# The last tile of a mixture of experts: its inner values in halves, its outputs in two transfers

## The chip, the cores and the metric

The kernel runs on one core of a Trainium2 chip. The metric is the device time of one execution in microseconds; three runs of the kernel before gave a median of 1152.88 us (1152.04 to 1154.29).

## The reference

A transformer block on x, 8 x 112 tokens of 512 channels. First x + tanh(g) * attention(layernorm(x)) with self and cross attention in simulated fp8, then a mixture of eight experts of which every token takes two:

```python
x = x + jnp.tanh(g_ffn[0]) * _L0_ffn_ref(_layernorm(x, axis=-1), Wr, Wg, Wu, Wd)

def _L0_ffn_ref(x, Wr, Wg, Wu, Wd):
    probs = jax.nn.softmax(x @ Wr, axis=-1)
    topk_w, topk_idx = jax.lax.top_k(probs, K)            # K = 2 of E = 8
    topk_w = topk_w / jnp.sum(topk_w, axis=-1, keepdims=True)
    for i in range(E):
        sel = topk_idx == i
        w_i = jnp.sum(topk_w * sel.astype(x.dtype), axis=-1, keepdims=True)
        h = jax.nn.silu(x @ Wg[i]) * (x @ Wu[i])
        output = output + w_i * (h @ Wd[i])
    return output
```

## The kernel before

The program has two parts: attention (up to about 790 us), and the projection with the experts. The change is in the second, in its last ten microseconds.

The 896 tokens with two choices each give 1792 rows. They are sorted by expert into tiles of 128 rows. How many tiles an expert fills depends on the routing, so the program runs TI = 21 tiles (2 x 7 + 8 - 1), enough for any routing. Rows that hold no token read token 0 when gathered, and when added back carry an index beyond the last token, which the transfer leaves out (bounds_check).

Every tile i passes these steps, with fp32 values handled as a rounded half (hi) and a rest (lo) so that TensorE's fp32r products keep their precision:
- GpSimd gathers 128 rows (gather, L1496). TensorE transposes them into the PSUM bank p_x, ScalarE takes xh, TensorE subtracts it (rest_of_rows), ScalarE takes xl.
- TensorE makes the gate and up products into the banks pg and pu, 12 matmuls of 512 columns each: four blocks k, three pairs of halves (products, L1748). ScalarE evacuates them (gated, L1586; upward, L1592), GpSimd multiplies them to hf (product, L1505).
- turn_inner (L1735): TensorE transposes hf into p_h. inner_high (L1598): ScalarE takes hh. rest_of_inner (L1741): TensorE subtracts it. inner_low (L1604): ScalarE takes hl.
- products again: the down product from hh and hl into the bank pd.
- result (L1612): ScalarE scales pd by the row's gate into y, of which there are two (y lies in the tile p_cat).
- add (L1511): GpSimd issues an indirect DMA that adds 128 rows of y into the output in memory (compute_op add).

Two adds must not be in flight at once, since two tiles may hold the same token: add(i) waits for `added`, the semaphore of the transfers' landing, to reach 16 * i. The order of the work is written out by hand, engine by engine, and software-pipelined: while TensorE makes tile i's gate and up products, the down product of tile i - 1 comes between, and ScalarE runs result(i - 1) before inner_high(i). For the last tile nothing is left to fill the gaps. The last statement of GpSimd's queue waits for the landing of the last add, and with that the program ends.

Of the kernel before, what the change touches and what calls it, by code (L numbers as in the profile page):

```python
# [21 lines left out]
ALU = mybir.AluOpType  # L22
ACT = mybir.ActivationFunctionType
AX = mybir.AxisListType.X

P = 128
B, T, D = 8, 112, 512
# [7 lines left out]
NT = B * T  # L35
EX, FF = 8, 512
FB = FF // P
# [3 lines left out]
TI = 2 * TJ + EX - 1  # L41
# [1212 lines left out]
def projected_experts(nc, c, sb, ps, sem, x, wproj, catd, W, Wr, ident, mhalf, proj_scale, gate,  # L1254
# [19 lines left out]
    hi, lo, l_done = ffn.hi, ffn.lo, ffn.l_done  # L1274
# [12 lines left out]
    def w_half(half, m):  # L1287

        return half[m // KB % 2][:, m % KB, :]

    def catr(m):
        return flat((hi, lo)[m // 2 % 2][2][:, 0:KB, :])[:, m % 2 * NT:(m % 2 + 1) * NT]

# [25 lines left out]
    of_row = sb(c, "of_row", [P, 2, TI], U32)  # L1319
    gate_of = sb(c, "gate_of", [P, 2, TI])  # L1320
# [12 lines left out]
    minus = sb(c, "minus", [P, P], F32R)  # L1333
# [5 lines left out]
    y = in_odd(0, 2 * D, F32).rearrange("p (r d) -> p r d", r=2)  # L1339
    lane_hot = in_odd(4 * D, CH * P, BF16).rearrange("p (n l) -> p n l", n=CH)  # L1340
    at = 4 * D + CH * P
# [11 lines left out]
    sg, up_out, hf = (results.held[:, 2 * k * FF:2 * (k + 1) * FF].bitcast(F32) for k in range(3))  # L1353
    hh = sb(c, "hh", [P, D], F32R)
    hl = sb(c, "hl", [P, D], F32R)

    p_count, p_rank, pg, pu, pd, p_x, p_h = (acc[:, j, :] for j in range(TJ))
    p_where = p_row[:, 0:2 * TI]
    p_share = p_row[:, 64:64 + 3 * TI]

# [95 lines left out]
    @block.gpsimd  # L1456
    def _(pool):
        pool.iota(expert_no[:, :], pattern=[[1, EX]], base=0, channel_multiplier=0,
                  allow_small_or_imprecise_dtypes=True).then_inc(pool_self, 1)
        pool.iota(tile_no[:, :], pattern=[[1, TI]], base=0, channel_multiplier=0,  # L1460
                  allow_small_or_imprecise_dtypes=True).then_inc(pool_self, 1)
        pool.iota(lane_no[:, :], pattern=[[1, P]], base=0, channel_multiplier=0,
                  allow_small_or_imprecise_dtypes=True).then_inc(pool_self, 1)
        pool.iota(block_row[:, :], pattern=[[P, TJ]], base=0, channel_multiplier=0,
                  allow_small_or_imprecise_dtypes=True).then_inc(pool_self, 1)
        pool.iota(block_no[:, :, :], pattern=[[0, 2], [1, TJ]], base=1, channel_multiplier=0,
                  allow_small_or_imprecise_dtypes=True).then_inc(pool_self, 1)
        pool.iota(part_no[:, :], pattern=[[0, 1]], base=0, channel_multiplier=1,
                  allow_small_or_imprecise_dtypes=True).then_inc(pool_self, 1)
        pool.memset(le[:, :, :], 1.0).then_inc(pool_self, 1)  # L1470
        pool.memset(tri[:, :], 1.0).then_inc(pool_self, 1)
        pool.memset(ones_bf[:, :], 1.0).then_inc(pool_self, 1)
        pool.memset(ends[:, 0:1], 0.0).then_inc(pool_self, 1)
        pool.wait_ge(pool_self, 10)
        pool.affine_select(out=le[:, :, :], in_=le[:, :, :], compare_op=ALU.is_ge, fill=0.0, base=0,
                           pattern=[[1, EX], [-1, EX]], channel_multiplier=0).then_inc(pool_self, 1)
        pool.affine_select(out=tri[:, :], in_=tri[:, :], compare_op=ALU.is_gt, fill=0.0, base=0,
                           pattern=[[1, P]], channel_multiplier=-1).then_inc(pool_self, 1)

        pool.memset(block_row[:, 0:1], -1.0).then_inc(const_done, 1)  # L1480
        pool.wait_ge(pool_self, 12)
        pool.tensor_scalar(minus[:, :], ident[:, :], -1.0, None, ALU.mult).then_inc(const_done, 1)
        pool.tensor_copy(tri_bf[:, :], tri[:, :]).then_inc(const_done, 1)
        pool.tensor_copy(lane_bf[:, :], lane_no[:, :]).then_inc(const_done, 1)

        for j in range(TJ):
            one = slice(j, j + 1)
            pool.wait_ge(stat_done, j + 1)
            pool.tensor_tensor(rstd[:, one], mv[:, j, 1:2], mhalf[:, 0:1], ALU.pow).then_inc(rstd_pow, 1)
            pool.wait_ge(rstd_pow, j + 1)  # L1490
            pool.tensor_tensor(shift[:, one], mv[:, j, 0:1], rstd[:, one], ALU.mult).then_inc(rstd_done, 1)

        def gather(i):
            if i >= 3:
                pool.wait_ge(tx_rdy, i - 2)
            pool.indirect_dma_start(  # L1496
                out=xr[:, i % 3, :], out_offset=None, in_=normed[:, :],
                in_offset=bass.IndirectOffsetOnAxis(ap=of_row[:, 0, i:i + 1], axis=0)).then_inc(xr_in[i % 3], 16)

        def product(i):  # L1500
            pool.wait_ge(sg_done, i + 1)
            pool.wait_ge(up_done, i + 1)
            if i >= 1:
                pool.wait_ge(th_rdy, i)
            pool.tensor_tensor(hf[:, :], sg[:, :], up_out[:, :], ALU.mult).then_inc(hf_done, 1)  # L1505

        def add(i):
            pool.wait_ge(y_done, i + 1)
            if i >= 1:
                pool.wait_ge(added, 16 * i)  # L1510
            pool.indirect_dma_start(  # L1511
                out=tokens[:, :], out_offset=bass.IndirectOffsetOnAxis(ap=of_row[:, 1, i:i + 1], axis=0),
                in_=y[:, i % 2, :], in_offset=None, bounds_check=NT - 1, oob_is_err=False,
                compute_op=ALU.add).then_inc(added, 16)

        pool.wait_ge(normed_kept, 32)
        pool.wait_ge(row_done, 1)
        for i in range(3):
            gather(i)
        pool.wait_ge(row_done, 2)  # L1520
        pool.wait_ge(out_kept, 32)
        for i in range(TI):
            product(i)
            if i >= 1:
                add(i - 1)
            if i + 3 < TI:
                gather(i + 3)
        add(TI - 1)
        pool.wait_ge(added, 16 * TI)

    @block.scalar
    def _(act):
# [61 lines left out]
        def inner_high(i):  # L1594
            act.wait_ge(th_rdy, i + 1)
            if i >= 1:
                act.wait_ge(dn_rdy, i)
            act.activation(hh[:, :], p_h[:, :], ACT.Copy).then_inc(hh_done, 1)  # L1598

        def inner_low(i):  # L1600
            act.wait_ge(sh_rdy, i + 1)
            if i >= 1:
                act.wait_ge(dn_rdy, i)
            act.activation(hl[:, :], p_h[:, :], ACT.Copy).then_inc(hl_done, 1)  # L1604

        def result(i):
            act.wait_ge(dn_rdy, i + 1)
            if i == 0:
                act.wait_ge(gate_done, 1)
            if i >= 2:  # L1610
                act.wait_ge(added, 16 * (i - 1))
            act.activation(y[:, i % 2, :], pd[:, :], ACT.Copy, scale=gate_of[:, 0, i:i + 1]).then_inc(y_done, 1)  # L1612

        rows_high(0)
        rows_low(0)
        for i in range(TI):
            gated(i)
            if i >= 1:
                inner_low(i - 1)
            upward(i)  # L1620
            if i + 1 < TI:
                rows_high(i + 1)
                rows_low(i + 1)
            if i >= 1:
                result(i - 1)
            inner_high(i)
        inner_low(TI - 1)
        result(TI - 1)

    @block.tensor  # L1630
    def _(pe):
# [98 lines left out]
        def turn_inner(i):  # L1730
            pe.wait_ge(hf_done, i + 1)
            if i >= 1:
                pe.wait_ge(hl_done, i)
            for k in range(FB):
                mm = pe.matmul(p_h[:, k * P:(k + 1) * P], hf[:, k * P:(k + 1) * P], ident[:, :],  # L1735
                               start=(k == 0), stop=False, is_transpose=True, skip_group_check=True)
            mm.then_inc(th_rdy, 1)

        def rest_of_inner(i):
            pe.wait_ge(hh_done, i + 1)  # L1740
            pe.matmul(p_h[:, :], minus[:, :], hh[:, :], start=False, stop=True,  # L1741
                      skip_group_check=True).then_inc(sh_rdy, 1)

        def products(bank, a_hi, a_lo, n, at, ks):
            for k in ks:
                for m in range(3):
                    a, w = ((a_hi, hi), (a_hi, lo), (a_lo, hi))[m]
                    mm = pe.matmul(bank[:, :], a[:, k * P:(k + 1) * P],  # L1748
                                   w[n][:, bass.ds(at + k, 1), :].rearrange("p a f -> p (a f)"),
                                   start=(k == 0 and m == 0), stop=(k == KB - 1 and m == 2))  # L1750
            return mm
# [35 lines left out]
                products(pd, hh[:, :], hl[:, :], 2, at.pop(i - 1), (2, 3)).then_inc(dn_rdy, 1)  # L1787
            turn_inner(i)
        rest_of_inner(TI - 1)
        pe.wait_ge(hl_done, TI)  # L1790
        pe.wait_ge(y_done, TI - 1)
        products(pd, hh[:, :], hl[:, :], 2, at.pop(TI - 1), range(FB)).then_inc(dn_rdy, 1)

    @block.vector
    def _(v):
# [214 lines left out]
```

## Time and profile before

| | |
|---|---|
| median of three runs | 1152.88 us (1152.04 to 1154.29) |
| profiled execution, its own time | 1152.41 us |
| its span | 1150.7 us |
| TensorE busy | 1086.5 us (94%) |
| ScalarE busy | 699.6 us (61%) |
| GpSimd busy | 501.8 us (44%) |

The span reaches from the first to the last event of the execution; some 1.7 us of its time lie outside it. PE is TensorE, PEld its weight loads, ACT ScalarE, DVE VectorE, POOL GpSimd, SP SyncE. Busy shares are means over the whole span and say nothing of its end; there, the chain of waits and the timeline are to be read. A duration of GpSimd's DMA_INDIRECT is the time in which GpSimd works on the instruction, not that of the transfer. Matmuls are pipelined: the start of one lies closer to the start of the next than its duration.

### The profile page before, as it was taken

What the parts mean: (1) busy time and instruction counts of PE and PEld (TensorE: products, weight loads), DVE (VectorE), ACT (ScalarE), POOL (GpSimd) and SP (SyncE); (2) the same over time, 40 slices, a digit from 0 to 9 for tenths busy, and PEclk for the clock granted to TensorE, in tenths of its full rate; (3) what the DMA queues carried; (4) which work ended last, traced back from release to release, by engine and by line L of the source; (5) the groups of instructions that cost most, each with busy time, mean ns of one, the idle gap of its engine ahead of it and who ended that gap; (6) DMA issues with size and microseconds to landing.
All of it is one profiled execution on the core that took longest, in us unless ns stands there. A gap on an engine that the chain in (4) does not pass through costs nothing. (4 is left out here: it accounts for less than half of the span.)

```text
span 1150.7 us, 19517 instructions
## 1 busy us (share of the span) xinstructions
PE 1086.5 (94%) x5662; PEld 891.0 (77%) x5662; DVE 779.8 (68%) x1558; ACT 699.6 (61%) x2032; POOL 501.8 (44%) x571
## 2 busy tenths in 40 slices
PE   4599999999999999999999999998999779999996
PEld 3488788888888788888887888886888657777785
DVE  7988986977776896777697766677454774655000
ACT  7668878666878856888867656763241323434432
POOL 3445565445544454445544554452000125565432
PEclk8799999999999999999999999999999879999999
DMA  7221111142111214121114111112944347673310
GB/s 265 106 69 48 49 36 45 36 154 90 44 37 44 62 36 181 44 54 36 44 36 135 63 45 36 46 34 94 351 157 147 129 151 217 182 239 97 54 43 0
DMA packets 52819, 107.39 MB, mean 93 GB/s; under 512 B 6064, under 2 KB 27056, under 8 KB 51184
## 3 DMA queue, kind: packets, MB, share of 16 engines
q1 hardware_dynamic: 48016, 97.00, 25.8%
q0 software_dynamic: 4704, 9.18, 3.5%
q8 instruction: 49, 0.80, 0.3%
q14 instruction: 50, 0.41, 0.1%
HBM read 91.48 MB, written 16.52 MB: 94 GB/s over the span
## 5 line engine op out<-in xcount | busy, mean ns | idle before, releaser
L529 POOL TENSOR_TENSOR c_lo<-c_raw,c_hi 128x500 fp32r<-128x500 f32 x96 | 124.0, 1292 | 194.0 <-ACT c_hi L581 194.0
L523 POOL TENSOR_TENSOR rs<-va,mhalf 125x2 f32<-125x2 f32 (+1 forms) x180 | 200.7, 1115 | 14.2 <-POOL va L516 0.2
L516 POOL TENSOR_TENSOR va<-ss,epst 125x2 f32<-125x2 f32 (+1 forms) x180 | 60.9, 338 | 179.4 <-DVE ss L1078 101.3
L798 PE MATMUL bank<-w_hi,c_hi 128*125 128x512 f32 x384 | 120.0, 434 | 8.2 <-ACT w_hi L576 6.9
L771 PE MATMUL bank<-w_hi,xqs 128*128 128x512 f32 (+2 forms) x464 | 111.1, 362 | 11.6 <-DVE xqs L1070 11.6
L798 PE MATMUL bank<-w_hi,c_lo 128*125 128x512 f32 x384 | 105.7, 397 | 0.0
L798 PE MATMUL bank<-w_lo,c_hi 128*125 128x512 f32 x384 | 105.1, 395 | 0.1
L771 PE MATMUL bank<-w_lo,xqs 128*128 128x512 f32 (+2 forms) x464 | 101.2, 340 | 0.1
L664 ACT ACTIVATE work<-bank,nmax 112x375 f32<-112x375 f32 x128 | 73.6, 584 | 44.9 <-DVE nmax L1107 44.8
L842 PE MATMUL bank<-kxT,qxT 128*112 128x375 f32 x256 | 97.0, 480 | 0.0
L771 PEld LDWEIGHTS bank<-w_hi,xqs 128*128 128x128 f32 (+1 forms) x464 | 74.1, 189 | 18.1 <-issue 12.2
L798 PEld LDWEIGHTS bank<-w_hi,c_hi 128*125 128x125 f32 x384 | 67.0, 188 | 26.5 <-issue 7.1
L798 PEld LDWEIGHTS bank<-w_hi,c_lo 128*125 128x125 f32 x384 | 71.7, 187 | 18.6
L798 PEld LDWEIGHTS bank<-w_lo,c_hi 128*125 128x125 f32 x384 | 71.2, 186 | 18.8 <-DVE w_lo L434 0.8
L771 PEld LDWEIGHTS bank<-w_lo,xqs 128*128 128x128 f32 (+1 forms) x464 | 75.3, 187 | 11.3 <-DVE w_lo L434 0.8
L873 PE MATMUL bank<-work 125*128 125x224 f32 x384 | 83.1, 352 | 0.0
L1133 DVE TENSOR_TENSOR results<-bank,smg 128x448 bf16<-128x448 f32 x64 | 39.9, 623 | 52.9 <-PE bank L873 52.9
L626 ACT ACTIVATE nkx<-bank 125x256 f32<-125x256 f32 x96 | 38.8, 404 | 58.6 <-PE bank L798 58.6
L873 PEld LDWEIGHTS bank<-work 125*128 125x128 f32 x384 | 72.4, 189 | 0.3
L1107 DVE TENSOR_REDUCE nmax<-bank 112x1 f32<-112x375 f32 x128 | 69.2, 543 | 3.0 <-PE bank L842 0.2
L1511 POOL DMA_INDIRECT out<-p_cat,of_row x21 | 45.5, 2167 | 58.2 <-ACT p_cat L1612 48.8
L856 PEld LDWEIGHTS bank<-ident,work 112*125 112x125 f32 x384 | 51.8, 188 | 19.2 <-issue 13.3
(266 smaller groups left out, 2798.7 us busy)
## 6 DMA issues: line engine op xcount, KB each, us to landing
c_raw<-in_ctxT SPq DMA_DIRECT2D x96, 250.0 KB, 2.6
shared<-in_w_in SPq DMA_DIRECT2D x13, 1024.0 KB, 9.2
shared<-in_wproj SPq DMA_DIRECT2D x32, 256.0 KB, 4.3
raw_g<-in_Wg SPq DMA_DIRECT2D x8, 1024.0 KB
raw_u<-in_Wu SPq DMA_DIRECT2D x8, 1024.0 KB, 6.2
raw_d<-in_Wd SPq DMA_DIRECT2D x8, 1024.0 KB, 5.4
cat_scratch<-results SPq DMA_DIRECT2D x32, 224.0 KB, 2.0
shared<-cat_scratch SPq DMA_DIRECT2D x2, 1792.0 KB, 9.4
```

The costliest lines, as they stand in the source:

```text
L516: pool.tensor_tensor(va[0:rows, lo:hi], ss[0:rows, lo:hi], epst[0:rows, lo:hi], ALU.add).then_inc(va_done, 1)
L523: pool.tensor_tensor(rs[0:rows, lo:hi], va[0:rows, lo:hi], mhalf[0:rows, lo:hi], ALU.pow).then_inc(rs_done, 1)
L529: pool.tensor_tensor(flat(c_lo[:, k, :, :]), flat(c_raw[:, k, :, :]), flat(c_hi[:, k, :, :]).bitcast(F32), ALU.subtract).then_inc(cl_done, 1)
L664: act.activation(pcross[0:T, h, :], p_cross[0:T, h % 2, 0:TC], ACT.Exp, bias=nmax[0:T, 4 + h:5 + h], accum_out=lsum[0:T, 4 + h:5 + h]).the ...
L771: m = pe.matmul(out, xqs[:, n, k, 0:rows], (w_hi, w_lo)[i // KB][:, k, lo:lo + w], start=(i == 0), stop=(i == 2 * KB - 1))
L798: m = pe.matmul(bank[0:CT, :], a[:, ch, k, :], w[:, k, CKX:CV], start=(i == 0), stop=(i == 3 * KB - 1))
L842: pe.matmul(p_cross[0:T, h % 2, 0:TC], qxT[:, t[1] % 2, h, :], kxT[:, h // HPG, :], start=True, stop=True).then_inc(sx_rdy, 1)
L856: m = pe.transpose(p_tr[0:CT, 1 - h % 2, k * T:(k + 1) * T], pcross[0:T, h, k * CT:(k + 1) * CT], ident[0:T, 0:T])
L873: m = pe.matmul(out[:, HPG * T:2 * HPG * T], valx[0:CT, par, k, g * P:(g + 1) * P], flat(pcrossT[0:CT, k, HPG * g:HPG * (g + 1), :]), star ...
L1107: v.tensor_reduce(nmax[0:T, 4 + h:5 + h], p_cross[0:T, h % 2, 0:TC], AX, ALU.max, negate=True).then_inc(mx_done, 1)
L1133: v.tensor_tensor(results.y[lin(t) % 2][:, g * 4 * T:(g + 1) * 4 * T].rearrange("p (a t) -> p a t", t=T), out_bank(t, g)[:, 0:4 * T].rearr ...
L1511: pool.indirect_dma_start(out=tokens[:, :], out_offset=bass.IndirectOffsetOnAxis(ap=of_row[:, 1, i:i + 1], axis=0), in_=y[:, i % 2, :], in ...
```

## The change

It concerns the last tile, TI - 1 = 20, alone.

- inner_banks: the transposes of its four blocks go to two banks, the first two to p_h, the last two to p_x. hh, the subtraction and hl are done in two halves of 256 columns each.
- Its down product goes to the banks pg (columns 0 to 255) and pu (256 to 511), one after the other, with 12 matmuls of 256 columns for each. It waits for both halves of hl.
- result makes y in two halves, each when its bank is ready. The result of tile 19 no longer comes before hh of tile 20 but behind hl.
- GpSimd waits for the landing of the first 20 adds, and then issues two indirect adds, one for each half of the columns, the second with no wait for the first's landing, since they don't meet.

```diff
+    def inner_banks(i):
+
+        if i < TI - 1:
+            return ((p_h, slice(0, FF)),)
+        return ((p_h, slice(0, FF // 2)), (p_x, slice(FF // 2, FF)))
...
+    OUT_BANKS = ((pg, slice(0, D // 2)), (pu, slice(D // 2, D)))
...
-        add(TI - 1)
-        pool.wait_ge(added, 16 * TI)
+        pool.wait_ge(added, 16 * (TI - 1))
+        for n, (bank, cols) in enumerate(OUT_BANKS):
+            pool.wait_ge(y_done, TI + n)
+            pool.indirect_dma_start(
+                out=tokens[:, :], out_offset=bass.IndirectOffsetOnAxis(ap=of_row[:, 1, TI - 1:TI], axis=0),
+                in_=y[:, (TI - 1) % 2, cols], in_offset=None, bounds_check=NT - 1, oob_is_err=False,
+                element_offset=n * (D // 2), compute_op=ALU.add).then_inc(added, 16)
+        pool.wait_ge(added, 16 * (TI + 1))
...
-            act.activation(hh[:, :], p_h[:, :], ACT.Copy).then_inc(hh_done, 1)
+            for bank, cols in inner_banks(i):
+                act.activation(hh[:, cols], bank[:, cols], ACT.Copy).then_inc(hh_done, 1)
...
+            for n, (bank, cols) in enumerate(inner_banks(i)):
+                act.wait_ge(sh_rdy, i + 1 + n)
+                if i >= 1:
+                    act.wait_ge(dn_rdy, i)
+                act.activation(hl[:, cols], bank[:, cols], ACT.Copy).then_inc(hl_done, 1)
...
-            act.activation(y[:, i % 2, :], pd[:, :], ACT.Copy, scale=gate_of[:, 0, i:i + 1]).then_inc(y_done, 1)
+            if i < TI - 1:
+                act.activation(y[:, i % 2, :], pd[:, :], ACT.Copy, scale=gate_of[:, 0, i:i + 1]).then_inc(y_done, 1)
+                return
+            for n, (bank, cols) in enumerate(OUT_BANKS):
+                act.wait_ge(dn_rdy, TI + n)
+                act.activation(y[:, i % 2, cols], bank[:, cols], ACT.Copy,
+                               scale=gate_of[:, 0, i:i + 1]).then_inc(y_done, 1)
...
-            if i >= 1:
+            if 1 <= i < TI - 1:
                 result(i - 1)
             inner_high(i)
         inner_low(TI - 1)
+        result(TI - 2)
         result(TI - 1)
...
+            for n, (bank, cols) in enumerate(inner_banks(i)):
+                pe.wait_ge(hh_done, i + 1 + n)
+                pe.matmul(bank[:, cols], minus[:, :], hh[:, cols], start=False, stop=True,
+                          skip_group_check=True).then_inc(sh_rdy, 1)
...
-        pe.wait_ge(hl_done, TI)
-        pe.wait_ge(y_done, TI - 1)
-        products(pd, hh[:, :], hl[:, :], 2, at.pop(TI - 1), range(FB)).then_inc(dn_rdy, 1)
+        pe.wait_ge(hl_done, TI + 1)
+        for bank, cols in OUT_BANKS:
+            for k in range(FB):
+                for m in range(3):
+                    a, w = ((hh, hi), (hh, lo), (hl, hi))[m]
+                    mm = pe.matmul(bank[:, cols], a[:, k * P:(k + 1) * P],
+                                   w[2][:, bass.ds(at[TI - 1] + k, 1), cols].rearrange("p a f -> p (a f)"),
+                                   start=(k == 0 and m == 0), stop=(k == FB - 1 and m == 2))
+            mm.then_inc(dn_rdy, 1)
```

On ScalarE, the end of the queue before (results are the gate and up values, the two p_cat rows are y of tiles 19 and 20):

```order
L1592 ACTIVATE results<-p_acc 128x512 [waits hf_done,u_rdy]
L1612 ACTIVATE p_cat<-p_acc,gate_of 128x512 [waits added,dn_rdy]
L1598 ACTIVATE hh<-p_acc 128x512 [waits dn_rdy,th_rdy]
L1604 ACTIVATE hl<-p_acc 128x512 [waits dn_rdy,sh_rdy]
L1612 ACTIVATE p_cat<-p_acc,gate_of 128x512 [waits added,dn_rdy]
```

And in the changed kernel:

```order
L1605 ACTIVATE results<-p_acc 128x512 [waits hf_done,u_rdy]
L1612 ACTIVATE hh<-p_acc 128x256 [waits dn_rdy,th_rdy]
L1612 ACTIVATE hh<-p_acc 128x256
L1619 ACTIVATE hl<-p_acc 128x256 [waits dn_rdy,sh_rdy] x2
L1628 ACTIVATE p_cat<-p_acc,gate_of 128x512 [waits added,dn_rdy]
L1632 ACTIVATE p_cat<-p_acc,gate_of 128x256 [waits dn_rdy,added]
L1632 ACTIVATE p_cat<-p_acc,gate_of 128x256 [waits dn_rdy]
```

y of tile 19 (128x512) has moved from before hh to behind both halves of hl, and y of tile 20 has become two.

On GpSimd, the end of the queue before (out is the output, p_cat holds y; a DMA row shows the whole output's shape):

```order
L1505 TENSOR_TENSOR results<-results 128x512 [waits th_rdy,up_done,sg_done]
L1511 DMA out<-p_cat,of_row 896x512 [waits added,y_done2] x2
L100 UNCONDITIONAL_BRANCH [waits added]
```

And in the changed kernel:

```order
L1512 TENSOR_TENSOR results<-results 128x512 [waits th_rdy,up_done,sg_done]
L1518 DMA out<-p_cat,of_row 896x512 [waits added,y_done2]
L1538 DMA out<-p_cat,of_row 896x512 [waits y_done2,added]
L1538 DMA out<-p_cat,of_row 896x512 [waits y_done2]
L100 UNCONDITIONAL_BRANCH [waits added]
```

Behind the last hf there are three adds in place of two; the second waits for the landing of the one before (added), the third for its half of y alone.

## Rows read from the trace of the kernel before

**Rows 1.** The page: busy time, share of the span and instructions of each engine.

```profile
PE 1086.5 (94%) x5662; PEld 891.0 (77%) x5662; DVE 779.8 (68%) x1558; ACT 699.6 (61%) x2032; POOL 501.8 (44%) x571
```

**Rows 2.** Busy time by stretch: PE, PEld, DVE, ACT, POOL (instructions), TensorE clock, DMA share, GB/s.

```profile
1137.00:1145.70 8.70, 3.94 (x17) 2.52 (x15) 0.00 (x0) 2.46 (x4) 3.14 (x2) 0.98 0.01 0
1145.70:1150.70 5.00, 0.00 (x0) 0.00 (x0) 0.00 (x0) 0.00 (x0) 0.00 (x0) 0.50 0.01 0
```

**Rows 3.** The chain of waits at the end: start us, us, what.

```profile
1138.23 0.51 PE p_acc L1741
...
1138.76 0.61 ACT hl L1604
...
1139.49 3.06 PE p_acc L1748 x12
...
1142.57 0.70 ACT p_cat L1612
...
1143.32 0.72 issue
1144.04 1.57 POOL out L1511
```

**Rows 4.** DMA answer from 1138.4 us to the end: packets and bytes.

```profile
DMA packets 288, 0.00 MB, mean 0 GB/s; under 512 B 288, under 2 KB 288, under 8 KB 288
```

**Rows 5.** DMA answer from 1099.9 to 1109.7 us: queue, packets, MB, share.

```profile
q0 software_dynamic: 224, 0.51, 28.3%
```

**Rows 6.** Timeline of GpSimd: start us, us, engine, line, operation, [idle before, releaser].

```profile
1099.96 1.59 POOL L1511 DMA_INDIRECT out<-p_cat,of_row  x1 [3.03 <-ACT p_cat L1612]
...
1138.46 1.57 POOL L1511 DMA_INDIRECT out<-p_cat,of_row  x1 [2.26 <-ACT p_cat L1612]
1144.04 1.57 POOL L1511 DMA_INDIRECT out<-p_cat,of_row  x1 [4.01 <-ACT p_cat L1612]
```

**Rows 7.** Timeline of TensorE and ScalarE at the end.

```profile
1136.80 0.60 PE L1735 MATMUL p_acc<-ident,results 128*128 128x128 f32 x4
1137.00 0.69 ACT L1612 ACTIVATE p_cat<-p_acc,gate_of 128x512 f32<-128x512 f32 x1 [2.21 <-PE p_acc L1748]
...
1141.91 0.40 PE L1748 MATMUL p_acc<-lo_d,hh 128*128 x1
1142.14 0.39 PE L1748 MATMUL p_acc<-hi_d,hl 128*128 x1
```

**Rows 8.** Timeline of ScalarE: copies of 256 columns out of PSUM.

```profile
49.64 0.39 ACT L619 ACTIVATE val<-bank 112x256 f32<-112x256 f32 x1 [0.27 <-PE bank L771]
49.92 0.38 ACT L621 ACTIVATE nk<-bank 128x256 f32<-128x256 f32 x1
```

**Rows 9.** Timeline of TensorE: matmuls of 256 columns, four in a row.

```profile
322.68 0.64 PE L771 MATMUL bank<-w_lo,xqs 128*128 128x256 f32 x4
323.15 0.63 PE L771 MATMUL bank<-w_hi,xqs 128*112 128x256 f32 x4
```

**Rows 10.** Groups of weight loads by form: busy us, mean ns.

```profile
L771 PEld LDWEIGHTS bank<-w_lo,xqs 128*128 128x128 f32 x336 | 58.5, 192 | 11.3 <-DVE w_lo L434 0.8
...
L1748 PEld LDWEIGHTS p_acc<-hi_d,hh 128*128 128x128 f32 x84 | 15.8, 188 | 8.0 <-issue 6.0
```

**Rows 11.** Busy time by stretch, around the packets of tile 19's add.

```profile
1140.80:1140.90 0.10, 0.10 (x2) 0.10 (x1) 0.00 (x0) 0.00 (x0) 0.00 (x0) 1.00 0.07 1
1140.90:1141.00 0.10, 0.10 (x2) 0.05 (x2) 0.00 (x0) 0.00 (x0) 0.00 (x0) 1.00 0.00 0
```

**Rows 12.** Busy time by stretch, at the end of the first gather's packets.

```profile
925.20:925.40 0.20, 0.00 (x0) 0.00 (x0) 0.17 (x1) 0.00 (x0) 0.20 (x1) 0.50 0.27 103
```

**Rows 13.** Timeline of TensorE: what waited for the first gather.

```profile
925.89 1.11 PE L1721 MATMUL p_acc<-ident,shared 128*128 128x128 f32 x4 [5.20 <-DMA shared<-normed_rows,of_row]
```

**Rows 14.** Timeline of GpSimd: a gather right behind a gather.

```profile
923.83 0.95 POOL L1496 DMA_INDIRECT shared<-normed_rows,of_row  x1 [0.30 <-issue]
```

**Rows 15.** Timeline of GpSimd: an add that waited for the landing of another.

```profile
971.72 1.64 POOL L1511 DMA_INDIRECT out<-p_cat,of_row  x1 [1.97 <-DMA out<-p_cat,of_row]
```

More of the change, by code:

```diff
@@ L1597, in inner_high @@
                 act.wait_ge(dn_rdy, i)
-            act.activation(hh[:, :], p_h[:, :], ACT.Copy).then_inc(hh_done, 1)
+            for bank, cols in inner_banks(i):
+                act.activation(hh[:, cols], bank[:, cols], ACT.Copy).then_inc(hh_done, 1)
         def inner_low(i):
-            act.wait_ge(sh_rdy, i + 1)
-            if i >= 1:
-                act.wait_ge(dn_rdy, i)
-            act.activation(hl[:, :], p_h[:, :], ACT.Copy).then_inc(hl_done, 1)
+            for n, (bank, cols) in enumerate(inner_banks(i)):
[3 more added lines that the diff above has]
+                act.activation(hl[:, cols], bank[:, cols], ACT.Copy).then_inc(hl_done, 1)
         def result(i):
@@ L1623, in _ @@
                 rows_low(i + 1)
-            if i >= 1:
+            if 1 <= i < TI - 1:
                 result(i - 1)
@@ L1733, in turn_inner @@
                 pe.wait_ge(hl_done, i)
+            banks = inner_banks(i)
             for k in range(FB):
-                mm = pe.matmul(p_h[:, k * P:(k + 1) * P], hf[:, k * P:(k + 1) * P], ident[:, :],
-                               start=(k == 0), stop=False, is_transpose=True, skip_group_check=True)
+                bank = banks[k * len(banks) // FB][0]
+                mm = pe.matmul(bank[:, k * P:(k + 1) * P], hf[:, k * P:(k + 1) * P], ident[:, :],
+                               start=(k * len(banks) % FB == 0), stop=False, is_transpose=True,
+                               skip_group_check=True)
             mm.then_inc(th_rdy, 1)
         def rest_of_inner(i):
-            pe.wait_ge(hh_done, i + 1)
-            pe.matmul(p_h[:, :], minus[:, :], hh[:, :], start=False, stop=True,
-                      skip_group_check=True).then_inc(sh_rdy, 1)
+            for n, (bank, cols) in enumerate(inner_banks(i)):
+                pe.wait_ge(hh_done, i + 1 + n)
+                pe.matmul(bank[:, cols], minus[:, :], hh[:, cols], start=False, stop=True,
+                          skip_group_check=True).then_inc(sh_rdy, 1)
         def products(bank, a_hi, a_lo, n, at, ks):
```

## The prediction

> **What bounds the kernel now.** I began with the busy shares of the page [rows 1]: TensorE holds 94% of the span. The slices after 1137 us tell another story: TensorE is busy 3.94 of the 8.70 us from 1137.00 to 1145.70, and in the last 5.00 us no engine is busy at all [rows 2]. So the end of the program is a chain of hand-overs, and the change touches only that end. The chain of waits [rows 3] gives it step by step: TensorE's transposes of the last tile, ScalarE's hh (the rounded inner values), TensorE's remainder product, ScalarE's hl (the rest), twelve products on TensorE (3.06 us), ScalarE's scaled copy into y (0.70 us), 0.72 us in which GpSimd gets the indirect add under way, and 1.57 us of GpSimd for the add itself. That ends at 1145.61; the span ends at 1150.7, so 5.1 us follow, for the landing of the add and the end of the program.
>
> The DMA answer from 1138.4 us on [rows 4] is what decides the case. The last two adds together move 288 packets and 0.00 MB. With these inputs the last tiles hold no token, and their rows are out of bounds. The add of 1099.96 us, in whose stretch 0.51 MB were moved (half of it by a gather of 128 rows of 2 KB), still took 1.59 us of GpSimd, against 1.57 us for an empty one [rows 5, 6]. What is split at the end is therefore a fixed cost and no data.
>
> **The change part by part.** All times are on the axis of the profiled execution.
>
> *Inner values in halves.* The transposes end at 1137.40 [rows 7]; hh now follows at once, at 1137.44 (such a hand-over takes 0.02 to 0.04 us in the chain), since the scaled copy of tile 19, which held ScalarE from 1137.00, has moved behind hl. A copy of 256 columns takes 0.39 us, and the next starts 0.28 us after it [rows 8]. The halves of hh are thus 1137.44 to 1137.83 and 1137.72 to 1138.11. The remainder product takes 0.51 us at 512 columns from a standing start [rows 3]; streamed, one of 512 columns starts 0.23 us behind the last [rows 7] and one of 256 some 0.118 us (the next four start 0.47 us behind four) [rows 9], so I take 0.51 - 0.12 = 0.39. The first half of the rest is in PSUM at 1138.26, the second at 1138.54. Then hl: 1138.28 to 1138.67, and 1138.56 to 1138.95. Before, hl ended at 1139.36. This part brings the products forward by 0.4 us.
>
> *Products in two halves of columns.* They are 24 of 256 columns in place of 12 of 512: 24 x 0.118 = 2.83 us against 12 x 0.233 = 2.80 (the twelve of the chain with their slower first one: 3.06). From 1139.07 the first half is ready at about 1140.7 and the second at about 1142.15, against 1142.55 before. The products' weight loads show 0.188 us each, longer than 0.118, and each is preceded by register work for the weights' place; if that holds them to the old pace, the halves take 24 x 0.233 = 5.6 us, and the second is ready at about 1144.85. But the row of 256 columns carries loads of 0.192 us too [rows 10] and still keeps 0.118, so I take that.
>
> *Results of the last tile.* A scaled copy of 256 columns should take 0.69 - 0.60 + 0.39 = 0.48 us. The first half of y is ready at 1141.2, the second at 1142.65, against 1143.26 before.
>
> *The result of tile 19 is moved.* This is the step that costs. It ran at 1137.00; now it stands behind both copies of hl, so it starts at 1138.84 and y is ready at 1139.53, 1.84 us later than 1137.69. GpSimd starts an add 0.77 us after y (1143.27 to 1144.04 [rows 3]; 1137.69 to 1138.46 [rows 6, 7]), so the add of tile 19 is on GpSimd from 1140.30 to 1141.87, where it was from 1138.46 to 1140.03.
>
> *The wait for the adds.* GpSimd waits for the landing of the add of tile 19 before it issues the first half for tile 20. Before, this was hidden: the add's last packet is seen by 1140.9, 0.87 us after GpSimd was done [rows 11], and the next y came at 1143.26. Now GpSimd frees itself at 1141.87 and y (first half) has long been there at 1141.2, so the landing is what ends last. Its length is not in the trace. From below it is 0.87 us; the first gather shows up to 0.5 us more, since its packets thin out by 925.4 and TensorE starts on it at 925.89 [rows 12, 13]; from above it is 3.2 us, because the last add began only 0.77 us after its own y, so the landing was over by 1143.3. I take 1.2 us, between 0.87 and 0.87 + 0.5, since those rest on rows that show packets. Queued behind this wait stand both halves' adds and the final wait, hence the end of the kernel. The Trainium skill, page "DMA: Bandwidth & Descriptors", section "Anatomy of one DMA", gives about 2.0 us as fixed for a GpSimd DMA, mostly the receipt of the write. By that figure, put in as the landing, the sum below would be 0.8 us larger; no row here shows it.
>
> *Two adds in place of one.* Landing at 1143.07, start 0.77 us later at 1143.84, done at 1145.41. The second half's y is there since 1142.65, so the two adds stand back to back. Back to back, GpSimd's indirect transfers start 0.30 us after the end of the one before [rows 14], so from 1145.71 to 1147.28. If the start-up of 0.77 us is not hidden behind the first, 0.47 us come on top. That each half costs a whole 1.57 us I take from full and empty adds costing the same [rows 5, 6]; the trace has no add of 256 columns, and half of it, 0.8 us, is the other bound. Below nothing it can't be, since the second add has to follow the first.
>
> *Sum.* GpSimd's last instruction ends at 1147.28 against 1145.61: +1.67 us. In two steps: GpSimd sat idle for 4.01 us before the last add [rows 6], and 1140.03 + 1.84 + 1.2 + 0.77 = 1143.84 fits in just before the old start, -0.20; the second add gives +0.30 + 1.57 = +1.87. 5.1 us follow as before. The profiled execution took 1152.41 us (1.71 outside its span); with +1.67 it is 1154.1. The median of the runs is 0.47 above the profiled one, 1152.88, and that is the one compared: 1154.5 us (+1.6 to +1.7). TensorE and ScalarE have slack in this sum: the second half's y may come as late as 1144.9 before anything shifts.
>
> **The rivals.**
>
> *The landing is long.* Its place is GpSimd's wait for the 20th add, its price one for one beyond 1.2 us. From 1.85 us on the kernel is slower by over 2.3 us; at the upper bound of 3.2 us it is +3.7, 1156.6. For it: real adds earlier landed late (the add of 971.72 waited for the one before) [rows 15]. Against it: those moved data beside weight loads, this one moves none, and its packets are through in 0.87 us. The Trainium skill's figure named above would put the kernel in this case, at +2.5, 1155.3.
>
> *The halves are cheap, and the result is no slower.* If GpSimd's time goes with the width, each add takes 0.8 us: with a landing of 0.87 us the first runs from 1143.5 to 1144.3 and the second from 1144.6 to 1145.4, 0.2 us before the old end: 1152.7. For it: the instruction moves half as many bytes. Against: 1.57 us without bytes and 1.59 us with them.
>
> *The kernel is faster by over 2.3 us.* The last transfer would have to be done before its y can be there: even with y of the second half at 1142.65, start at 1143.42 and a cheap add of 0.8 us, GpSimd ends at 1144.2, which is -1.4 us. From this chain it can't come, only from the scatter.
>
> *The products don't keep 0.118 us.* At 0.233 us the second y is ready at 1145.35 and its add runs from 1146.1 to 1147.7: +2.1, 1155.0. This matters only from 1144.9 on, so most of it is hidden.
>
> **How the numbers follow.** Forecast (+1.3 to +2.2) 0.58; long landing or start-up not hidden (+2.3 to +3.7) 0.20; slow products 0.05; cheap halves (-0.3 to +0.9) 0.15; faster by more 0.02. A median of this kernel can't be told from no change below about 0.2%, 2.3 us (three runs spread over 2.25 us). The forecast lies inside that bound by 0.6 us, so part of its chance, through the scatter of the medians, goes to slower: slower 0.27, same 0.69, faster 0.04. The range takes in both sides of the cases and the scatter of about 1 us: 1152.6 to 1156.6.
>
> **What would show it.** Right: ScalarE's rows in the order hh, hh, hl, hl, y, y, y; y of tile 19 ending near 1139.5; GpSimd's idle time before the first half's add put down to the DMA; two adds of 1.57 us with 0.3 us between; the chain of waits ending on GpSimd twice; some 5.1 us behind. Wrong: an add of 0.8 us, the first half's add starting 0.77 us after its y (then the landing did not bind), gaps in the products of 256 columns, or a tail after the last add that differs from 5.1 us.

## The result, and the profile after

The changed kernel takes 1154.77 us (median of 21 runs, 1153.74 to 1157.2) against 1152.70 us for the kernel before (21 runs, 1151.42 to 1155.4). The ratio is 1.0015, with a 95% interval of 1.0009 to 1.0021: slower by 1.7 us, between 1.0 and 2.4. (The two medians themselves lie 2.07 us apart.) The forecast was 1154.5 us.

The chain of waits of the changed kernel, from the copy of hh on, answers to [rows 3] (start us, us, what):

```profile
1137.80 0.39 ACT hh L1612
1138.19 0.04 issue
1138.23 0.40 PE p_acc L1767
...
1138.95 0.36 ACT hl L1619
1139.32 0.59 ACT p_cat L1628
...
1139.96 0.72 issue
1140.67 2.89 DMA out<-p_cat,of_row
...
1144.34 1.57 POOL out L1538
1145.91 0.30 issue
1146.21 1.56 POOL out L1538
```

The products, which made up 3.06 us of the old chain, are no longer in it. The chain now runs through the copy of tile 19, its add, and the landing of that add (2.89 us from its start), and then through two adds. The timeline shows what went on beside it; its rows answer to [rows 6, 7]:

```profile
1137.16 0.60 PE L1759 MATMUL p_acc<-ident,results 128*128 128x128 f32 x4
...
1138.66 0.66 ACT L1619 ACTIVATE hl<-p_acc 128x256 fp32r<-128x256 f32 x2 [0.20 <-PE p_acc L1767]
1139.21 0.68 ACT L1628 ACTIVATE p_cat<-p_acc,gate_of 128x512 f32<-128x512 f32 x1
1139.44 0.36 PE L1821 MATMUL p_acc<-hi_d,hh 128*128 x1 [0.55 <-ACT hl L1619]
1139.64 0.28 PE L1821 MATMUL p_acc<-lo_d,hh 128*128 x1
1139.75 0.28 PE L1821 MATMUL p_acc<-hi_d,hl 128*128 x1
...
1140.67 1.57 POOL L1518 DMA_INDIRECT out<-p_cat,of_row  x1 [4.10 <-ACT p_cat L1628]
...
1141.21 0.47 ACT L1632 ACTIVATE p_cat<-p_acc,gate_of 128x256 f32<-128x256 f32 x1 [1.32 <-PE p_acc L1821]
...
1142.54 0.47 ACT L1632 ACTIVATE p_cat<-p_acc,gate_of 128x256 f32<-128x256 f32 x1 [0.85 <-PE p_acc L1821]
1144.34 1.57 POOL L1538 DMA_INDIRECT out<-p_cat,of_row  x1 [2.09 <-DMA out<-p_cat,of_row]
1146.21 1.56 POOL L1538 DMA_INDIRECT out<-p_cat,of_row  x1 [0.30 <-issue]
```

The first half of y is there at 1141.68 and the second at 1143.01, and still GpSimd sits idle for 2.09 us between the add of tile 19 and the next: 1.33 us until that add has landed, and 0.77 us to start. Ahead of the last tile's transposes the change leaves everything as it was, but the whole end of the program slides by up to 3 us from one execution to the next. So all that follows is counted from T, the end of the last tile's transposes: 1137.40 before, 1137.76 after, and 1136.72 in a second profile of the changed kernel. GpSimd's last instruction ends at T + 8.21 before (1145.61) and at T + 10.01 after (1147.77): +1.80 us. Behind it stand 5.09 us before and 5.13 after. On the axis of the profiles GpSimd ends 2.16 us later; the remaining 0.36 us is the shift of T. The changed kernel itself shows T at both sides of 1137.40, so I take that shift for no effect of the change.

### The profile page after: what moved, and what is told of

Same layout as the page of the kernel before. It is cut to its first block and busy times, and to the rows that moved or that the text cites. A ratio compares the mean times of both kernels' runs of the same rounds, so it can differ in the third digit from the quotient of the medians.

```text
span 1152.9 us, 19556 instructions
## 1 busy us (share of the span) xinstructions
PE 1088.3 (94%) x5675; PEld 893.3 (77%) x5675; DVE 780.1 (68%) x1558; ACT 699.5 (61%) x2035; POOL 501.2 (43%) x572
## 5 line engine op out<-in xcount | busy, mean ns | idle before, releaser
L1518 POOL DMA_INDIRECT out<-p_cat,of_row x20 | 43.0, 2150 | 56.9 <-ACT p_cat L1628 43.6
```

## The experiments

One table of all runs. T, GpSimd's end (from T) and the tail (from there to the end of the span) come from one profile each, the medians from 21 runs of the first two kernels and 11 or 12 of the others (5 of e5); the ratio is to the kernel before, with its 95% interval. The span is printed to 0.1 us, so a tail is good to 0.05 us. The groups e1 to e4, e5 to e8 and e9 to e12 each ran beside the kernel before, whose median was 1152.90, 1152.49 and 1153.85 us there: across groups, compare ratios and not medians.

| kernel | T | GpSimd's end, from T | tail | median us | ratio |
|---|---|---|---|---|---|
| before | 1137.40 | 8.21 | 5.09 | 1152.70 | 1 |
| changed | 1137.76 | 10.01 | 5.13 | 1154.77 | 1.0015 (1.0009 to 1.0021) |
| changed, again | 1136.72 | 9.86 | 5.12 | 1153.60, one run | - |
| e1, one add | 1137.62 | 7.97 | 5.11 | 1153.23 | 0.9999 (0.9986 to 1.0012) |
| e2, y of tile 19 back | 1139.34 | 8.35 | 5.11 | 1153.91 | 0.9997 (0.9987 to 1.0008) |
| e3, both | 1138.57 | 7.82 | 5.11 | 1152.27 | 0.9992 (0.9980 to 1.0004) |
| e4, two adds alone | 1139.70 | 10.14 | 5.16 | 1155.48 | 1.0017 (1.0004 to 1.0029) |
| e5, four adds alone | 1138.91 | 13.88 | 5.31 | 1158.45 | 1.0048 (1.0033 to 1.0064) |
| e6, data, one add | 1137.52 | 8.27 | 7.31 | 1154.89 | 1.0019 (1.0009 to 1.0029) |
| e7, data, changed | 1137.11 | 10.71 | 6.28 | 1156.46 | 1.0033 (1.0022 to 1.0044) |
| e12, e7 again | 1138.01 | 10.77 | 6.32 | 1156.86, one run | - |
| e8, y of tile 19 moved alone | 1138.59 | 8.74 | 5.07 | 1153.93 | 1.0008 (0.9999 to 1.0017) |
| e9, hh products first | 1137.73 | 7.20 | 5.07 | 1152.19 | 0.9988 (0.9975 to 1.0000) |
| e10, e3 and hh products first | 1136.87 | 8.04 | 5.09 | 1151.67 | 0.9983 (0.9973 to 0.9994) |

**e1: one add in place of two.**

```diff
-        for n, (bank, cols) in enumerate(OUT_BANKS):
-            pool.wait_ge(y_done, TI + n)
-            pool.indirect_dma_start(... in_=y[:, (TI - 1) % 2, cols] ...)
+        pool.wait_ge(y_done, TI + 1)
+        pool.indirect_dma_start(... in_=y[:, (TI - 1) % 2, :] ...)
...
```

Expected: 

> The changed kernel with one add of 512 columns for the last tile in place of two of 256; inner values, products and copies stay in halves, and the result of tile 19 stays behind hl. Times are counted from the end of the last tile's transposes (T) to the end of GpSimd's last instruction: before 8.21 us, changed 10.01 us. Theory (the second add is what costs, 1.87 us): the landing of tile 19's add comes at T + 5.8, the one add starts at T + 6.6 and ends at T + 8.15, so 0.1 us below the kernel before and 1.9 below the changed one: about 1152.7 us. Rival (the halves of products and copies, or the wait for the landing, cost the time): it stays at T + 9.5 or more, about 1154.5 us.

Measured: T + 7.97, the theory. Its one add still waits for the DMA:

```profile
1140.53 1.57 POOL L1518 DMA_INDIRECT out<-p_cat,of_row  x1 [4.10 <-ACT p_cat L1627]
1144.02 1.57 POOL L1537 DMA_INDIRECT out<-p_cat,of_row  x1 [1.93 <-DMA out<-p_cat,of_row]
```

Of the 2.04 us below the changed kernel, 1.87 is the second add; the rest is a landing shorter by 0.17 us. The ratio, 0.9999, agrees, but its interval still touches that of the changed kernel (1.0012 against 1.0009): the reading rests on the profile.

**e2: the result of tile 19 back in its old place.**

```diff
-            if 1 <= i < TI - 1:
+            if i >= 1:
                 result(i - 1)
...
         inner_low(TI - 1)
-        result(TI - 2)
```

Expected: 

> The changed kernel with the result of tile 19 put back before hh of tile 20; both halves of everything, two adds. Theory: tile 19's add lands at T + 4.0, before the first half of y (T + 4.1), so the wait for it goes; the adds run from T + 4.85 and T + 6.7, and the second, which stands right behind the first, ends at T + 8.3: +0.1 us on the kernel before, about 1152.8 us. Of the 1.87 us of the second add the two seconds by which the first half's y is earlier hide nearly all. Rival (the second add costs its 1.87 us wherever it stands): T + 9.9 to 10.1, about 1154.6 us.

Measured: T + 8.35, again the theory. GpSimd's timeline:

```profile
1140.40 1.57 POOL L1518 DMA_INDIRECT out<-p_cat,of_row  x1 [2.26 <-ACT p_cat L1628]
1144.25 1.57 POOL L1538 DMA_INDIRECT out<-p_cat,of_row  x1 [2.27 <-ACT p_cat L1632]
1146.13 1.56 POOL L1538 DMA_INDIRECT out<-p_cat,of_row  x1 [0.30 <-issue]
```

The first half's add is now released by its own y (at T + 4.1) and starts at T + 4.91 in place of T + 6.58. The second add is there as before, and the end is only 0.14 us later than in the kernel before. So undoing either part alone brings back the whole loss. The 1.87 us of the second add are hidden by the time that the first half gains, and the late add of tile 19 takes that time away.

**e3: both undone, the halves of the computation left.**

Expected: 

> Both of these: the changed kernel with one add of 512 columns and the result of tile 19 in its old place. What is left of the change are the halves of the inner values, products and copies. Theory: y is complete at T + 5.4 against T + 5.87 before, so GpSimd ends at T + 7.75, 0.45 us below the kernel before: about 1152.3 us, too little to be told by the times, but not by the trace. Rival (halves of the inner values gain nothing, the wait between the engines is what counts): T + 8.2, 1152.7 us.

Measured: T + 7.82. The last add waits for y again, and not for the DMA:

```profile
1144.82 1.57 POOL L1537 DMA_INDIRECT out<-p_cat,of_row  x1 [3.62 <-ACT p_cat L1631]
```

The halves of inner values, products and copies are thus worth 0.39 us by the profiles; the interval of the ratio takes in 1, so the times don't show it. This run is also the right base for e1 and e2, which have these halves too. From T + 7.82, the moved copy alone costs 0.15 us (e1), the second add alone 0.53 us (e2), and both together 2.19 us (2.04 in the second profile of the changed kernel). Together they cost about 1.4 to 1.5 us more than the sum of the two.

**e4: the kernel before with its last add cut in two.**

```diff
-        add(TI - 1)
+        pool.wait_ge(added, 16 * (TI - 1))
+        pool.wait_ge(y_done, TI)
+        for n in range(2):
+            cols = slice(n * (D // 2), (n + 1) * (D // 2))
+            pool.indirect_dma_start(... in_=y[:, (TI - 1) % 2, cols] ..., element_offset=n * (D // 2) ...)
...
```

Expected: 

> The kernel before with the last add alone cut into two of 256 columns, both behind the whole y. Theory: nothing hides the second add, so +0.30 + 1.57 = +1.87 us: T + 10.1, about 1154.6 us. Rival (two adds overlap, or the tail behind them gets shorter with half the width): under +1 us, below 1153.7 us.

Measured: T + 10.14, +1.93 us; the tail behind it is 5.16 us, no shorter than that behind one add. GpSimd's timeline:

```profile
1146.40 1.57 POOL L1532 DMA_INDIRECT out<-p_cat,of_row  x1 [4.06 <-ACT p_cat L1619]
1148.28 1.56 POOL L1532 DMA_INDIRECT out<-p_cat,of_row  x1 [0.30 <-issue]
```

So the second add does not need the moved copy to cost its full price. Here both adds wait for the whole y, nothing comes earlier, and nothing is hidden. In unrounded times of the traces the tail is 5.06 to 5.07 us behind one empty add, 5.13 to 5.14 behind two and 5.32 behind four: more adds make it slightly longer.

**e5: the same with four adds of 128 columns.**

Expected: 

> The kernel before with the last add cut into four of 128 columns, all behind the whole y. Theory (a fixed price for each indirect instruction, whatever its width): +3 x 1.87 = +5.6 us, T + 13.8, about 1158.3 us, each 1.57 us on GpSimd. Rival (GpSimd's time goes in part with the width): instructions of 128 columns clearly below 1.57 us, and below +5 us in all.

Measured: T + 13.88, +5.67 us, three times 1.89. GpSimd's timeline:

```profile
1145.61 1.57 POOL L1532 DMA_INDIRECT out<-p_cat,of_row  x1 [4.07 <-ACT p_cat L1619]
1147.49 1.56 POOL L1532 DMA_INDIRECT out<-p_cat,of_row  x1 [0.30 <-issue]
1149.35 1.57 POOL L1532 DMA_INDIRECT out<-p_cat,of_row  x1 [0.30 <-issue]
1151.23 1.56 POOL L1532 DMA_INDIRECT out<-p_cat,of_row  x1 [0.30 <-issue]
```

An indirect add of 128 rows takes 1.56 to 1.57 us of GpSimd at 512, 256 and 128 columns, with no data at any of these widths, and with data at 512 and 256 (e6, e7). The bound of 0.8 us for a half, and the rival of cheap halves with it, are ruled out.

**e6 and e7: the last tile with tokens.** Does the split lose only because the last tile is empty here? Both kernels send the last add to the tokens of tile 0. Their output is then not the reference's; they show times alone, and tile 19 stays empty in them.

```diff
-                out=tokens[:, :], out_offset=bass.IndirectOffsetOnAxis(ap=of_row[:, 1, TI - 1:TI], axis=0),
+                out=tokens[:, :], out_offset=bass.IndirectOffsetOnAxis(ap=of_row[:, 1, 0:1], axis=0),
```

Expected of the kernel before with it: 

> The kernel before, but its last add sends the rows of the last tile to the tokens of tile 0, so that it carries 128 rows of 2 KB in place of none (the sums it adds there are not the reference's). Theory: GpSimd's 1.57 us stay (T + 8.2), and the tail behind it grows from 5.1 us by x, the movement of 0.26 MB with its reading and adding, 1 to 3 us: 1153.7 to 1155.7 us. Rival (the tail is fixed at 5.1 us): 1152.7 us.

Expected of the changed kernel with it: 

> The changed kernel with the same edit: both halves of the last add go to the tokens of tile 0 and carry data (the sums it adds there are not the reference's). Theory: the second half's add still ends GpSimd at T + 10.0, and only half of x is left behind it, since the first half moves while GpSimd works on the second: +1.8 - x / 2 against the run with one add and data, so still slower as long as x is below 3.6 us. Rival (the split pays where the last tile holds tokens): equal to that run or faster.

Measured: the data make the tail 7.31 us long behind one add, x = 2.2 us, and 6.28 behind two halves. The split thus saves 1.03 us there, half of x as expected, against 1.8 that it costs. The medians say +1.57 us for the split and the profiles +1.41, more than the 0.7 expected. Of that, 0.68 us is the landing of tile 19's add, 2.01 us here against 1.33 in the changed kernel:

```profile
1144.38 1.57 POOL L1538 DMA_INDIRECT out<-p_cat,of_row  x1 [2.79 <-DMA out<-p_cat,of_row]
```

Even with tokens in the last tile the split does not pay: with the landing of 1.16 us that most profiles show, the same sum would still give +0.56. The times alone are less firm, since the intervals of the two ratios overlap (1.0009 to 1.0029 against 1.0022 to 1.0044). A tile 19 with tokens was not run.

**e12: e7 once more.** Expected: 

> The changed kernel with data in the last add once more (the sums it adds there are not the reference's). If the landing of tile 19's add is long because of something in this kernel, 2.0 us again and GpSimd's end at T + 10.7; if by chance, 1.2 to 1.4 us and T + 10.0. Both halves' data leave a tail of 6.3 us either way.

Measured: T + 10.77 and a tail of 6.32 us, as the first time, with a landing of 2.08 us. By the expectation this speaks for a cause in this kernel and against chance; the last section has what the traces show of it.

**e8: the kernel before with y of tile 19 moved alone.**

```diff
-            if i >= 1:
+            if 1 <= i < TI - 1:
                 result(i - 1)
             inner_high(i)
         inner_low(TI - 1)
+        result(TI - 2)
```

Expected: 

> The kernel before with the result of tile 19 alone moved behind hl of tile 20; nothing in halves, one last add. Theory: tile 19's add starts at T + 3.2, ends at T + 4.8 and lands at T + 6.1, while y of tile 20 is complete at T + 5.7; the last add starts at T + 6.9 and ends at T + 8.45: +0.2 us, about 1152.9 us, with the wait put down to the DMA. Rival (the landing takes longer than 1.33 us, or the move is free since GpSimd idled for 4 us): +0.8 us or more, or -0.15 us.

Measured: T + 8.74, and not through the wait that I had named. TensorE's and GpSimd's rows:

```profile
1141.21 0.47 PE L1749 MATMUL p_acc<-hi_d,hh 128*128 x1 [1.45 <-ACT p_cat L1612]
...
1145.76 1.57 POOL L1511 DMA_INDIRECT out<-p_cat,of_row  x1 [2.44 <-ACT p_cat L1612]
```

Here the last products go into the bank pd, which tile 19's copy has to empty first, so TensorE itself waited for the moved copy, and y came at T + 6.40 instead of T + 5.7. I had overlooked that wait. In the changed kernel it can't arise, since its products go to other banks; there the use of pg and pu is what the move needs. The 0.53 us of this run are therefore the price of another wait than that of the changed kernel.

**e11: the changed kernel once more, for the landing.** Expected: 

> The changed kernel once more, for the landing of tile 19's add, which took 1.33 us from the end of GpSimd's instruction in its profile, 1.16 in the run with one add and 2.0 in the run with data in the last add. If it is a fixed time, 1.2 to 1.4 us and GpSimd's end at T + 10.0; if it scatters by itself, anything up to 2 us, one for one on GpSimd's end.

Measured: the landing of tile 19's add took 1.16 us from the end of GpSimd's instruction, and GpSimd ended at T + 9.86.

```profile
1139.64 1.57 POOL L1518 DMA_INDIRECT out<-p_cat,of_row  x1 [4.10 <-ACT p_cat L1628]
1143.14 1.57 POOL L1538 DMA_INDIRECT out<-p_cat,of_row  x1 [1.93 <-DMA out<-p_cat,of_row]
```

The same program thus gave 1.33 and 1.16 us: the landing is not one fixed time.

**e9: the products that need hh alone come first.** The chain suggested this: in the last tile eight of the twelve products need no hl, and stand behind the wait for it.

```diff
-        pe.wait_ge(hl_done, TI)
         pe.wait_ge(y_done, TI - 1)
-        products(pd, hh[:, :], hl[:, :], 2, at.pop(TI - 1), range(FB)).then_inc(dn_rdy, 1)
+        for k, m in [(k, m) for k in range(FB) for m in (0, 1)] + [(k, 2) for k in range(FB)]:
+            if (k, m) == (0, 2):
+                pe.wait_ge(hl_done, TI)
+            a, w = ((hh, hi), (hh, lo), (hl, hi))[m]
+            mm = pe.matmul(pd[:, :], a[:, k * P:(k + 1) * P], ...
```

Expected: 

> The kernel before, with the last tile's twelve products in another order: the eight that need hh alone first, and only the four with hl behind the wait for hl. Nothing in halves. Theory (the last tile is a chain of hand-overs, so work that waits for nothing should fill them): the products start after the remainder product, at T + 1.4 in place of T + 2.1, with hl copied beside them; GpSimd ends at T + 7.5 against T + 8.2: about 1152.0 us. Rival (ScalarE's copy of hl or the weight loads hold TensorE back as before): T + 8.1 to 8.2.

Measured: T + 7.20, 1.01 us below the kernel before, and more than the 0.7 us expected. Its chain:

```profile
1138.56 0.50 PE p_acc L1741
1139.06 2.81 PE p_acc L1795 x12
1141.87 0.02 issue
1141.89 0.70 ACT p_cat L1612
...
1143.36 1.57 POOL out L1511
```

The copy of hl and its two hand-overs have left the chain. The times say 0.9988 (0.9975 to 1.0000), in keeping with 1.01 us, 0.09%.

**e10: e3 with the same order of products.**

```diff
+        for parts in ((0, 1), (2,)):
+            if parts == (2,):
+                pe.wait_ge(hl_done, TI + 1)
+            for bank, cols in OUT_BANKS:
+                for k in range(FB):
+                    for m in parts:
...
```

Expected: 

> The same order of the products put into the changed kernel, with the result of tile 19 in its old place and one add: inner values in halves, the hh products of both halves of columns first, then the hl products of the first and of the second half. Theory: hh products from T + 1.25, y complete at T + 4.7, the one add ends at T + 7.05, 1.15 us below the kernel before: about 1151.6 us, on the edge of what the times can tell. Rival (tile 19's add lands only after T + 4.7 and takes the place of the wait, as it did in the changed kernel): T + 7.4 or more, with GpSimd's idle time put down to the DMA.

Measured: 1151.67 us, 0.9983 (0.9973 to 0.9994), so faster than the kernel before and the changed one. It has the lowest ratio of all, but its interval overlaps those of e9 and e3, and the times don't tell these three apart. And its profile shows the rival, not the theory. y was complete at T + 4.74, as expected, and then GpSimd waited:

```profile
1140.75 0.86 ACT L1631 ACTIVATE p_cat<-p_acc,gate_of 128x256 f32<-128x256 f32 x2 [2.19 <-DMA out<-p_cat,of_row]
1143.34 1.57 POOL L1537 DMA_INDIRECT out<-p_cat,of_row  x1 [3.83 <-DMA out<-p_cat,of_row]
```

In this execution tile 19's add landed 3.06 us after GpSimd's instruction, and GpSimd ended at T + 8.04, not 7.05; that its span is short is owed to an early T. With a landing of 1.16 us it would have come at T + 3.8, ahead of y, and the add would have ended near T + 7.1, as expected. How often the landing is late, and so how much of the 1.15 us this version gains on average, the one profile doesn't tell.

## Why the prediction was right

- *Inner values in halves.* Forecast: hl complete at T + 1.55. Measured: T + 1.55 (1139.31).
- *Products.* They kept 0.12 us from start to start (1139.64, 1139.75), and the second half's y came at T + 5.25, as forecast. The first half's came at T + 3.92, against 3.8: the second product started 0.20 us behind the first (1139.44, 1139.64) in place of 0.12, which I had left out. It changed nothing, since that half was not what ended last. The rival of slow products fell; by the prediction's own sum it would have added 0.4 us.
- *The result of tile 19.* Forecast and measured: y at T + 2.13.
- *The landing.* Forecast 1.2 us, measured 1.33: from 1142.24 to 1143.57, and 1.16 in the second profile. The packets themselves were through 0.8 us after the instruction, as before:

```profile
1142.80:1142.90 0.10, 0.00 (x0) 0.00 (x0) 0.00 (x0) 0.10 (x1) 0.00 (x0) 1.00 0.20 3
1142.90:1143.00 0.10, 0.00 (x0) 0.00 (x0) 0.00 (x0) 0.10 (x1) 0.00 (x0) 1.00 0.40 6
1143.00:1143.10 0.10, 0.00 (x0) 0.00 (x0) 0.00 (x0) 0.01 (x1) 0.00 (x0) 1.00 0.11 2
```

  Some 0.5 us lie between the last packet and the release, as at the first gather [rows 12, 13], and 0.3 us in the second profile. The prediction said that the trace has no length for this landing. It has one: the transfer raises the semaphore added by 16 in sixteen single steps, the trace keeps the time of each, and in the kernel before the last of them came 1.17 us after GpSimd's instruction. The 1.2 us were a choice inside bounds, and they met the value that most profiles show. That no late landing fell into the profile of the changed kernel is luck: with the 3.06 us of e10, GpSimd would have ended 1.7 us later, and the profile would have shown the rival of the long landing. The 2.0 us by the Trainium skill's page "DMA: Bandwidth & Descriptors", section "Anatomy of one DMA", is too long as a landing for these two profiles (1.33, 1.16); the two with data in the last add came to it (2.01 and 2.08), but there fifteen of the sixteen steps had come by 1.16 us.
- *Two adds.* 1.57 + 0.30 + 1.56 us, start-up hidden, as forecast; e4 and e5 show that price to be the same at 256 and 128 columns.
- *Sum.* +1.67 us forecast, +1.80 in the profile counted from T (1.65 in the second one), 1.7 in the ratio.
- *The noise.* This was put too high. The prediction took 0.2%, 2.3 us, as the least that medians can tell, from three runs. Twenty-one runs of each gave an interval of 1.0 to 2.4 us, clear of zero, so they could tell +1.7 us from no change.

One thing was told badly. The prediction called the moved copy the step that costs, and then booked -0.20 us for it and +1.87 for the second add, as if these were separate prices. Beside the halves, e1, e2 and e3 show that they are not: 0.15 us for the moved copy, 0.53 us for the second add, 2.19 us for both. The second add costs its full price wherever nothing hides it (e4, 1.93 us). The halves gave it something to hide behind, and the moved copy took that away.

## What to carry to other kernels

Before a last transfer is cut in two, ask whether its price lies in the bytes or in the instruction, and vary the width to see: here a second indirect add costs 1.87 us of GpSimd, and letting half of 128 full rows go earlier was worth 1.03. When two edits meet at one wait, undo each alone and then both, since part of the loss may belong to the pair, and the run with both undone is the base to count from. At the end of a pipeline, where nothing fills the gaps any more, look first for work that stands behind a wait it doesn't need: reordering twelve products gave 1.01 us by the profiles, all the halves 0.39. The times don't separate the two.

## What the runs showed of the hardware that I had not expected

The landing of the same empty add scattered, from 1.16 to 3.06 us after the end of GpSimd's instruction. The sixteen steps by which it raises added tell more than the last one alone, and they are in all fourteen traces, also where nobody waited for them. In every trace fifteen of them had come by 1.16 us. In ten traces the sixteenth had come by 1.17 us too. In the other four it was late, and these are the four in which a 16 KB packet of the instruction queue (q8 in the DMA view) was running at some time between 0.7 us before the end of GpSimd's instruction and 1.16 us after it. All times of this table are counted in us from that end:

| kernel | packet of 16 KB, start to end | sixteenth step |
|---|---|---|
| changed | -0.68 to 0.27 | 1.32 |
| e7, data | -0.33 to 0.96 | 2.01 |
| e12, e7 again | -0.33 to 1.02 | 2.07 |
| e10 | 0.83 to 2.01 | 3.06 |
| e3 | 1.56 to 2.67 | 1.16 |
| e2 | 1.78 to 3.07 | 1.16 |
| the other eight | none near | 1.16 to 1.17 |

The add's own packets show what happened in e10:

```profile
1140.10:1140.20 0.10, 0.10 (x3) 0.10 (x2) 0.00 (x0) 0.00 (x0) 0.00 (x0) 1.00 0.38 6
1140.20:1140.30 0.10, 0.10 (x3) 0.10 (x2) 0.00 (x0) 0.00 (x0) 0.00 (x0) 1.00 0.25 4
1140.30:1140.40 0.10, 0.10 (x3) 0.10 (x3) 0.00 (x0) 0.00 (x0) 0.00 (x0) 1.00 0.75 164
1141.50:1141.60 0.10, 0.00 (x0) 0.00 (x0) 0.00 (x0) 0.10 (x1) 0.00 (x0) 1.00 0.13 1
```

The last two columns are the DMA share and GB/s; the row with 164 GB/s is the instruction packet. The last row is nine packets of the add, by the DMA answer from 1141.4 to 1141.7 us. Nine of 144 is one sixteenth, as one step is of sixteen. They start as the instruction packet ends (1141.50 and 1141.52), and the sixteenth step follows 0.96 us behind the last of them. In e7 and e12, too, the last nine packets start as the instruction packet ends. So these nine stood behind it, which accounts for the three long landings. The short delay of the changed kernel (0.16 us), where the packet had ended before the add's packets began, is not explained. No run moved the instruction packet on purpose. It started at T + 4.16 in both runs with data, but at T + 3.8 in one profile of the changed kernel and at T + 16.2 in the other; what sets its time stays open.

T itself lay between 1136.7 and 1139.7 us in the profiles, with no relation to the edits; that is more than most of the effects here, and why they were read from T.
